# Two mixers of a graph-transformer kernel issued step by step between the turns of two edge stages, with relation sums added to X directly

## The reference

```python
# layer 1, graph step (relational): mean per (relation, destination), then a product per relation
h = segment_sum(x[src] * w[:, None], rel * N + dst) / max(count, 1)
out = einsum('rnc,rco->no', h.reshape(R, N, C), weight) + x @ root + bias
...
# layer 1, mixer (linear attention, 4 heads of 32, 4 memory rows)
q, k, v = split(rmsnorm(x, g_pre) @ w_qkv)
k, v = concat(memory_k, k), concat(memory_v, v)
q = softmax(q, over the 32 features of a head) * SCALE
k = softmax(k, over all nodes)
out = rmsnorm((q @ (k.T @ v)) @ w_out + b_out, g_out) + x
...
# layer 2, graph step (isomorphism): sum of the sources, then two products with batch norms
# layer 2, mixer: keys and values are x, centred and scaled per head of 32, with own weight and bias
out = x @ (k.T @ v / N) + x
```

## Time and profile before

| what | value |
|---|---|
| median of 3 runs | 7497.59 us (7496.27 to 7501.97) |
| profiled execution, its own time | 7498.07 us |
| its span, first to last instruction | 7496.4 us |
| mean granted TensorE clock | 0.777 |
| busy: TensorE / VectorE / ScalarE / GpSimd | 60% / 45% / 25% / 50% |
| instructions | 74035 |

### The profile page before, as it was taken

How to read it: one execution, slowest core, us unless ns; L and a number is a source line. 1 busy time by engine, 2 the same in 40 slices (tenths; PEclk the granted TensorE clock), 3 DMA queues, 4 the chain that set the end, 5 groups by cost and what they waited for, 6 DMA issues and landing times. The chain is left out here.

```text
span 7496.4 us, 74035 instructions
## 1 busy us (share of the span) xinstructions
PE 4494.6 (60%) x18035; PEld 3311.2 (44%) x18035; DVE 3397.3 (45%) x8025; ACT 1888.4 (25%) x4800; POOL 3731.6 (50%) x3581
## 2 busy tenths in 40 slices
PE   0160666666664791978864763555438965997528
PEld 0030444444443571356653652333237853665415
DVE  6840677777777314343336124332471115442361
ACT  0000555555554120023331110000102212442201
POOL 0776777777774363047750554775004433774300
PEclk9985777777776796977766886776769987996659
DMA  0020444444442472334360322336005642332400
GB/s 37 10 57 11 125 122 123 122 123 121 121 125 68 138 213 69 127 97 105 103 80 5 101 74 84 105 105 82 14 7 184 187 138 80 104 104 62 46 21 17
DMA packets 390998, 677.71 MB, mean 90 GB/s; under 512 B 127989, under 2 KB 257180, under 8 KB 387124
## 3 DMA queue, kind: packets, MB, share of 16 engines
q0 software_dynamic: 188992, 431.92, 23.7%
q1 hardware_dynamic: 201638, 241.74, 10.0%
HBM read 591.29 MB, written 81.90 MB: 90 GB/s over the span
## 5 line engine op out<-in xcount | busy, mean ns | idle before, releaser
L1209 POOL DMA_INDIRECT g0e_got<-g_table,g0e_rc x496 | 594.8, 1199 | 293.5 <-issue 157.0
L986 POOL DMA_INDIRECT g1e_got<-g_table,g1e_rc x496 | 485.1, 978 | 477.6 <-DMA g1e_rc<-rec_dst 326.9
L986 POOL DMA_INDIRECT g3e_got<-g_table,g3e_rc x496 | 490.0, 988 | 349.9 <-issue 142.4
L1211 POOL DMA_INDIRECT g0e_keyed<-g_keys,g0e_rc x496 | 572.2, 1154 | 166.6 <-issue 166.6
L986 POOL DMA_INDIRECT g2e_got<-g_table,g2e_rc x496 | 473.5, 955 | 261.1 <-issue 147.1
L1051 PE MATMUL g2e_pa<-g2e_got,g2e_placew 128*125 128x256 f32 x992 | 361.1, 529 | 323.4 <-issue 217.8
L257 POOL DMA_INDIRECT rec_dst<-bydst_rc,bydst_sloti x391 | 394.1, 1008 | 294.3 <-DVEq L449 175.4
L1273 PE MATMUL g0e_pt<-g0e_new,g0e_placet 125*128 125x8 f32 x992 | 211.0, 341 | 490.7 <-DVEq L1343 490.7
L1247 ACT ACTIVATE g0e_spaced<-g0e_spread 125x512 bf16<-125x512 f32 x992 | 499.1, 627 | 21.8 <-PE g0e_spread L1283 19.7
L2153 PE MATMUL f_p<-f_w2s,f_hid 128*128 128x256 f32 (+1 forms) x2176 | 493.1, 383 | 12.7 <-ACT f_hid L2173 1.7
L2142 PE MATMUL f_p<-f_xt,f_w1s 128*128 128x256 f32 (+1 forms) x2176 | 491.3, 383 | 14.4 <-DMA f_b2s<-in_L_ffn_b 8.9
(11 more groups left out here) (609 smaller groups left out, 8559.2 us busy)
## 6 DMA issues: line engine op xcount, KB each, us to landing
f_w1s<-in_L_ffn_W SPq DMA_DIRECT2D x32, 1024.0 KB, 5.7
f_w2s<-in_L_ffn_W SPq DMA_DIRECT2D x32, 1024.0 KB, 7.6
g_table<-g1t_out SPq DMA_DIRECT2D x25, 1000.0 KB
f_w1s<-in_L_ffn_w SPq DMA_DIRECT2D x40, 512.0 KB
f_w2s<-in_L_ffn_w SPq DMA_DIRECT2D x40, 512.0 KB
f_results<-f_y SPq DMA_DIRECT2D x72, 256.0 KB, 2.2
f_b2s<-in_L_ffn_b SPq DMA_DIRECT2D x80, 128.0 KB, 6.9
f_rows<-XN SPq DMA_DIRECT2D x3, 3125.0 KB
```

What stands on the lines that cost most here:

```text
L986: pool.indirect_dma_start(got[:, g % GOTS, j, :], None, table, bass.IndirectOffsetOnAxis(rc[:, g * GT + j, idx:idx + 1], 0))\
L1209: pool.indirect_dma_start(got[:, s, j, :], None, table, bass.IndirectOffsetOnAxis(rc[:, sl, j, R_IDX:R_IDX + 1], 0)).then_inc(got_in[s], 16)
L1211: pool.indirect_dma_start(keyed[:, s, j, :], None, keys, bass.IndirectOffsetOnAxis(rc[:, sl, j, R_KEY:R_KEY + 1], 0)).then_inc(got_in[s], 16)
```

## The change

The root product and the softmax mixer become `SoftmaxMixer`, the side of the relation stage; the head-norm mixer becomes `HeadNormMixer`, the side of the weighted-sum stage. The separate stages are gone. The relation stage adds its sums to X itself instead of a cleared accumulator. The identity is added into `root` and into the head-norm matrix `M`, so that XN comes with the product and has no addition of its own. Softened queries overwrite chunk 0 of XNT. Tiles are worked one after the other: the softmax mixer takes two turns per tile for projections, then one turn per two tiles for the keys, then one per tile for the output; the head-norm mixer takes two turns per tile and then one per tile.

```diff
+class HeadNormMixer:
+    START = 4
...
+    def tensor(self, pe):
+        for _ in range(self.START + 4):
+            yield
+        for t in range(NT):
+            pe.wait_ge(self.ready, t + 1)
+            for c in range(KC):
+                at = slice(c * 128, (c + 1) * 128)
+                last = pe.matmul(self.kv[c][:, 0:128], self.K[:, t % 2, at], self.V[:, t % 2, at], start=(t == 0),
+                                 stop=(t == NT - 1))
+            last.then_inc(self.multiplied, 1)
+            yield
+            yield
+        pe.wait_ge(self.have_m, 1)
+        for t in range(NT):
...
+            last.then_inc(self.made, 1)
+            yield
...
+class SoftmaxMixer:
+    START = 4
...
+    def sync(self, sp):
...
+                sp.dma_start(to, of).then_inc(self.loaded, 16)
+        sp.wait_ge(self.loaded, 16 * self.LOADS)
+
+    def tensor(self, pe):
+        for _ in range(self.START + 2):
+            yield
...
+        for t in range(NT):
+            rows = slice(t * P, (t + 1) * P)
+            if t > 0:
+                pe.wait_ge(self.a_taken, t)
+            for c in range(KC):
+                last = pe.matmul(self.A[0:P, 0:3 * HID], R.XNT[:, c, rows], self.w[:, c, :], start=(c == 0), stop=(c == KC - 1))
+            last.then_inc(self.a_made, 1)
+            yield
+            if t > 0:
+                pe.wait_ge(self.b_taken, t)
+            for c in range(KC):
+                last = pe.matmul(self.B[0:P, 0:D], R.XNT[:, c, rows], self.root[:, c, :], start=(c == 0), stop=(c == KC - 1))
+            last.then_inc(self.b_made, 1)
+            if t > 0:
+                turn(t - 1)
+            yield
...
+        pe.wait_ge(self.have_cmax, 1)
+        pe.wait_ge(self.a_taken, NT)
+        pe.transpose(self.A[:, 0:P], self.cmax[:, :], R.identf[0:P, 0:P]).then_inc(self.cmax_turned, 1)
+        yield
...
+    def scalar(self, act):
+        for _ in range(self.START - 2):
+            yield
+        for t in range(NT):
+            act.activation(self.junk[:, :], node_tile(R.XN, t), ACT.Square, accum_out=self.ss[:, t:t + 1])
+            act.drain()
+            if t % 12 == 11:
+                yield
...
+    def vector(self, dve):
+        for _ in range(self.START):
+            yield
+        dve.wait_ge(self.loaded, 16 * self.LOADS)
...
+        for t in range(NT):
+            if t > 0:
+                soften(t - 1)
+            project(t)
+            yield
+            root(t)
+            yield
+        soften(NT - 1)
+        dve.drain().then_inc(self.have_cmax, 1)
+        yield
+        yield
+        dve.wait_ge(self.cmax_turned, 1)
...
+        for t in range(NT):
+            dve.wait_ge(self.o_made, t + 1)
+            dve.tensor_tensor(self.o[:, t % 2, :], (self.A, self.B)[t % 2][0:P, 0:D], self.bout[:, :], ALU.add)
+            dve.drain().then_inc(self.o_biased, 1)
+            if t > 0:
+                finish(t - 1)
+            yield
+        finish(NT - 1)
...
-        rows_stage(nc, R, "g1root", w[:, :, :], D, finish_root,
-                   loads=[(w[:, :, :], chunks_of(a["L1_gnn_root"], D)), (b[:, :], row_of(a["L1_gnn_bias"], P))])
-    with ExitStack() as ctx:
-        acc = ctx.enter_context(nc.sbuf_tensor("g1_acc", [P, NT * D], F32))
-        edge_stage(nc, R, "g1e", "relation", by_dst, acc[:, :], D, table, idx=R_ROW, spread=R.inv_count[:, :])
-        add_stage(nc, [(R.X, acc)])
+        edge_stage(nc, R, "g1e", "relation", by_dst, R.X[:, :], D, table, idx=R_ROW, spread=R.inv_count[:, :],
+                   side=SoftmaxMixer(nc, R, ctx, a), clear=False)
...
-        edge_stage(nc, R, "g2e", "weight", by_dst, acc[:, :], D, table)
+        with ExitStack() as inner:
+            edge_stage(nc, R, "g2e", "weight", by_dst, acc[:, :], D, table, side=HeadNormMixer(nc, R, inner, a))
...
-            softmax_mixer(nc, R, "m1", a["L1_mix_w_qkv"], a["L1_mix_w_out"], a["L1_mix_b_out"], a["L1_mix_g_pre"],
-                          a["L1_mix_mem_kv"], a["L1_mix_g_out"])
...
-            head_norm_mixer(nc, R, a)
```

More of the change, by code:

```diff
@@ L2489, in relation_graph_layer @@
     with ExitStack() as ctx:
-        w = ctx.enter_context(nc.sbuf_tensor("g1_root", [128, KC, D], F32))
-        b = ctx.enter_context(nc.sbuf_tensor("g1_bias", [P, D], F32))
-        def finish_root(dve, t, ps, out):
-            x = node_tile(R.X, t)
-            dve.tensor_tensor(x, x, ps[:, 0:D], ALU.add)
-            dve.drain()
-            dve.tensor_tensor(x, x, b[:, :], ALU.add)
-        rows_stage(nc, R, "g1root", w[:, :, :], D, finish_root,
-                   loads=[(w[:, :, :], chunks_of(a["L1_gnn_root"], D)), (b[:, :], row_of(a["L1_gnn_bias"], P))])
-    with ExitStack() as ctx:
-        acc = ctx.enter_context(nc.sbuf_tensor("g1_acc", [P, NT * D], F32))
-        edge_stage(nc, R, "g1e", "relation", by_dst, acc[:, :], D, table, idx=R_ROW, spread=R.inv_count[:, :])
-        add_stage(nc, [(R.X, acc)])
+        edge_stage(nc, R, "g1e", "relation", by_dst, R.X[:, :], D, table, idx=R_ROW, spread=R.inv_count[:, :],
+                   side=SoftmaxMixer(nc, R, ctx, a), clear=False)
 def second_feed_forward(nc, R, a, spare):
@@ L3012, in program @@
         with nc.cleanup_on_exit():
-            softmax_mixer(nc, R, "m1", a["L1_mix_w_qkv"], a["L1_mix_w_out"], a["L1_mix_b_out"], a["L1_mix_g_pre"],
-                          a["L1_mix_mem_kv"], a["L1_mix_g_out"])
-        with nc.cleanup_on_exit():
             second_feed_forward(nc, R, a, by_src)
```

394 lines of the change are left out of this document (316 added, 78 removed).

## The result

The changed kernel takes 7193.4 us (median of 4 runs, 7192.3 to 7197.1) against 7497.3 us before: ratio 0.9596, 95% interval 0.9585 to 0.9608, 303.9 us less. The forecast was 7207 us.

The account below looks back on a forecast made before the run. GpSimd's issue of indirect gathers was taken to pace the relation and weighted-sum stages. 7498.1 - 327.1 + 25 (relation) + 2 (weighted sum) + 10 (gathers), less 0.5 for the median, gave 7207 us; range 7175 to 7295.

Parts of the forecast that it names:

- What goes away: Root product before the relation stage 33.2 us, addition stage and softmax mixer 170.3, head-norm mixer 123.6: 327.1 us.
- The squares: Relation stage: ScalarE squares 12 tiles in each of two early turns, 7.2 us, some 8 us late.
- the two same-turn waits: Relation stage, keys' maxima: in two turns VectorE waits for a product issued that same turn, 8 us in all.
- The projection turns: Relation stage: VectorE's turns of 6.3 and 4.4 us against GpSimd's 5.10 make 50 turns 13.5 us late.
- TensorE's 10 us for its lower clock: Relation stage: TensorE can't keep up at 1.2 GHz; projections like clock 0.98, output turns like 0.80; 10 us.
- The output turns: Relation stage: VectorE's 25 softmax output turns take 5.5 us each against GpSimd's 5.10, 10 us.
- Halved banks: Edge stages with a mixer: fewer placement, spread and sum banks cost nothing, as TensorE waits for VectorE's placement anyway.
- Weighted-sum stage and gathers: Weighted-sum stage takes back 2 us; gathers beside a mixer grow 10 ns each, 10 us over both stages.
- The same-turn chain: Rival: 25 softmax output turns take 9.5 us, as in the attention stage; 110 us instead of 10, 7307 us; chance 0.12.
- The shared path: Rival: gathers held while VectorE works on two operands in memory; 86 us instead of 10, 7283 us; chance 0.11.
- The slower case: Rival: every mixer turn is the same-turn chain, projections too, 12.6 us per projection turn; 7638 us; chance 0.03.
- All absorbed: Rival: TensorE reaches its higher level and the buffers absorb the stages' delays; 7180 us; chance 0.14.

Follow-up runs that it names:

- run 1: Changed kernel with its head-norm mixer as a separate stage again: 7312.7 us, ratio 0.9758.
- run 2: Kernel before with only the head-norm mixer moved beside the weighted-sum stage: 7379.0 us, ratio 0.9845.
- run 9: Kernel before with relation sums added to X directly, no accumulator, clearing or addition stage; slower third chip: 7953.4 us, ratio 0.9988.
- run 7: Run 6 with less VectorE projection work: ScalarE scales the values, TensorE adds the root's bias: 7167.5 us, ratio 0.9569.
- Run 6: Changed kernel with squares spread over four turns and waits around the keys' maxima set a turn apart: 7184.1 us, ratio 0.9588.
- Run 3: Kernel before with one placement, one spread and two sum banks in edge stages without a mixer: 7492.7 us, ratio 0.9998.
- run 4: Changed kernel with TensorE's 25 softmax output products issued one turn later, in the turn VectorE waits for them: 7317.3 us, ratio 0.9764.
- run 5: Changed kernel with VectorE taking the attention stage mixer's output products one turn behind TensorE: 7100.8 us, ratio 0.9479.
- run 10: Changed kernel with VectorE's 25 head-norm output steps one turn behind TensorE's products; slower third chip: 7688.7 us, ratio 0.9657.
- run 8: Changed kernel with two more unused two-operand SBUF products on VectorE in each head-norm key and value turn: 7237.8 us, ratio 0.9665.

## Why the prediction was right, and where it was off

**What goes away** was put at 327.1 us and measured 326.9. Runs 1 and 2 show the halves add up, run 9 the addition's own 9 us.

**The bound.** GpSimd's issue paces both stages: shown by the changed kernel (22.2 and 3.3 us of waiting) and by run 7, where the relation stage with its mixer is as short as without one.

**The relation stage: +17.8 us in place of 25 and 5 for its gathers.** The stage gave back more than was forecast, and of its terms some were right and some not.
- The clearing of the accumulator was counted at nothing. The prediction looked at when the first gather starts, not at how long it takes: 3.87 us, and 1.28 without the clearing, 2.6 us of the difference.
- The squares (7.1 and 6.9 us for twelve, measured) and the two same-turn waits (2.60 and 5.51 us, 8.1 together, put at 8) were sized right. Run 6 shows that only some 5 us of these reached the end.
- The projection turns were put at 6.3 and 4.4 us. Most took 6.38 and 4.34, as forecast. But their mean over all of the projections is 5.58, 24 us late in 50 turns where the term had 13.5.
- The other 11 us are mostly TensorE's, which the prediction had keeping up in these turns. In ten of them the sum took 3.05 to 3.76 us and VectorE's addition waited for it, 6.6 us in all beyond the usual 1.0 each; in all others the sum took 1.97. Waits for the spread and the projection make 2.0 more. Two sums one turn apart, the late addition, and TensorE's clock in a stretch within the second sum (length; busy and instructions of PE, PEld, DVE, ACT, POOL; clock, DMA share, GB/s):

```profile
3366.56 1.97 PE L1487 MATMUL g1e_pa<-g1e_got,g1e_placew 128*125 128x256 f32 x8
...
3372.93 3.56 PE L1487 MATMUL g1e_pa<-g1e_got,g1e_placew 128*125 128x256 f32 x8
...
3377.34 0.42 DVE L1557 TENSOR_TENSOR X<-X,g1e_pa 125x256 f32 x1 [1.97 <-PE g1e_pa L1487]
```

```profile
3374.00:3376.00 2.00, 2.00 (x6) 1.54 (x6) 1.11 (x4) 1.27 (x4) 1.39 (x3) 0.50 0.36 109
```

- So TensorE's 10 us for its lower clock were of the right size, some 8.6, and in the wrong place. They were meant for the output turns and rested on a clock of 0.80 there, and it was 0.88 from 3700 to 3800 us, against 0.80 before; GpSimd doesn't wait in these turns. The projections, which were to look like the attention stage's 0.98, had 0.89 to 0.96: the mean hides short falls to the lower level.
- The output turns took 5.41 us (put at 5.5), and their 0.3 x 25 = 8 us were paid by the twelve key turns of 4.15 us, which win back 11. I had set 8 against the whole and 10 beside it, so here 2 too many.

By these the sum is 8 + 24 + 8 - 17.5 = 22.5 us up to the last of the key maxima, and GpSimd waited some 17 there. Of the 37 us that the prediction let both stages and their gathers take back, 22.2 came, and nearly all of the forecast's 14 us of error lies in this stage. The total came out near because the 327 us could be read off the timeline, and because the 10 us for TensorE, set in the wrong place, were met by a loss of that size in another: that part was luck.

**Halved banks: nothing.** Run 3 shows it for the kernel before, run 7 beside the mixer.

**Weighted-sum stage and gathers.** +4.4 us for both together, where 2 + 5 stood; gathers +9 ns there and +4 ns in the relation stage for 10. Without its first gather, which the clearing no longer lengthens, the relation stage's are 972 ns before and 981 after, but 981 also in run 2, which has no mixer there: that growth isn't clear of the scatter. The weighted-sum stage's is, again without the first gather: 949 to 951 ns in the three kernels without a mixer there, 958 or 959 in the changed kernel and runs 2 and 4 to 7. The same-turn wait delays nobody there: GpSimd's 3.3 us of waiting show it, and run 10 agrees.

**The rivals.** The same-turn chain is real and was rightly left to others: the kernel issues the product a turn ahead, and run 4 shows what one turn less costs, 126 us where 110 - 10 stood. The error was to carry over 9.5 us a turn from a stage in which VectorE has a lighter turn (busy for 19 of 100 us there, for 32 in run 4). The shared path's price was added up wrongly: 0.29 x 3 + 0.42 + 0.29 + 0.84 is 2.4 us and not 2.0, so that rival stood for 94 us and 7291, still in the range. In that size it is refuted by run 8; the gathers grew by some 7 to 9 us. The slower case's figure of 12.6 us per projection turn was not tried. "All absorbed", 7180 us, is what runs 6 and 7 together reach: a ratio of 0.9569 is 7174 us beside the 7497.3 of the kernel before.

## What to carry to other kernels

Work set beside a stage that one engine's issue paces is nearly free as long as each other engine's turn, its own work and the guest's together, stays within that pace plus what the buffers hold once; count it engine by engine, turn by turn. Ahead of counting, look whether a guest step waits for a product of its own turn: where the host's next turn depends on the waiting engine, as in the relation and attention stages, one turn of distance is worth 90 to 130 us here, and where the host's inputs were made turns before, as in the weighted-sum stage, nothing of it was seen. Look for the same loop in stages that the change leaves alone: the largest gain beyond the change itself was there, 88 us.

## What the runs showed of the hardware that was not expected

**A gather is held by VectorE only at its start, and only by operations on SBUF.** From 3300 to 3500 us of the changed kernel ten gathers take 1.32 to 1.42 us in place of 0.95. All ten started within the stage's own 0.68 us placement, whose two inputs lie in SBUF. The additions of the sums, with one input in PSUM, hold nobody. One of each, from the timeline:

```profile
3303.82 0.68 DVE L1547 TENSOR_TENSOR g1e_place<-iota,g1e_rc 128x500 bf16<-128x500 f32 x1
3303.95 1.37 POOL L1422 DMA_INDIRECT g1e_got<-g_table,g1e_rc  x1 [0.30 <-issue]
...
3305.50 0.42 DVE L1557 TENSOR_TENSOR X<-X,g1e_pa 125x256 f32 x1 [1.00 <-issue]
3305.62 0.95 POOL L1422 DMA_INDIRECT g1e_got<-g_table,g1e_rc  x1 [0.31 <-issue]
```

The placement ends at 3304.50, the gather at 3305.32, 0.82 us later. So it is, within 0.01 us, for each of the sixteen gathers of this stretch that started 0.08 to 0.51 us into a placement (0.99 to 1.42 us long), and for eight that started in the first 0.12 us of one of the mixer's 0.29 us operations on two tiles in SBUF. Run 8 repeats it: the 38 gathers that started in the first 0.52 us of one of its added operations end 0.81 to 0.82 us after it. A gather that has its first 0.13 us behind it (0.95 - 0.82) goes on undisturbed, and so does VectorE beside it. Where both start within 0.02 us of each other, the gather isn't held and VectorE's operation takes 0.03 to 0.05 us longer. The clearing of an accumulator, which reads nothing, holds one too, in the kernel before in the relation stage and in the changed kernel in the weighted-sum stage, where it runs from 4389.22 for 5.39 us. The first gather of the stage ends 0.91 us after it in the first case and 0.93 in the second:

```profile
3251.61 5.39 DVE L1063 MEMSET g_acc<- 125x6400 f32 x1 [1.78 <-issue]
```

```profile
4391.60 3.94 POOL L1422 DMA_INDIRECT g2e_got<-g_table,g2e_rc  x1 [110.25 <-DMA g2e_rc<-rec_dst]
```

The Trainium skill's rule (SBUF — State Buffer, Who interferes with whom), that a VectorE operation with two SBUF inputs and a GpSimd instruction that reads SBUF exclude each other, is thus seen here, PSUM's exemption too, but for 0.13 us of each gather and not for its length. That is why 72 us of such work cost the gathers 9, and why the prediction's 86 us were so few.

**On the third chip the kernel before was 6% slower, and the time was lost in a few places.** Beside the trace of the kernel before, that of run 9 is 447 us longer: 152 us by the first gather of the first edge stage, and 87, 78 and 112 us in the relation, weighted-sum and attention gathers. Gathers were issued in the same 0.96 us there. What differs is a regular wait: nearly every second turn of GpSimd in the relation stage takes 6.7 us in place of 5.0, and every sixth in the weighted-sum stage, the number of its buffers, 8.9. One of each:

```profile
3506.80 0.94 POOL L986 DMA_INDIRECT g1e_got<-g_table,g1e_rc  x1 [1.97 <-DMA rec_src<-bysrc_rc,bysrc_sloti]
...
5111.19 0.94 POOL L986 DMA_INDIRECT g2e_got<-g_table,g2e_rc  x1 [4.27 <-DMA f_results<-f_y]
```

The transfers named as releasers belong to other stages, so what GpSimd waits for there wasn't settled. The relation stage's gathers spanned 722 us in place of 635 with no mixer at all, and 783 to 790 with one. That the mixer lengthens the stage by some 60 us there and by 19 on the faster chips says that the room beside the gathers is a property of the chip as well as of the kernel.
